# Writing the loop over units of edges out in full in a graph-convolution kernel

## What is computed

```
h   = x @ W_in2f
Wij = ssp(f_ij @ W_filt1 + b_filt1) @ W_filt2 + b_filt2      # f_ij: 200000 x 20
Wij = Wij * rcut_ij[:, None]
agg = segment_sum(h[idx_j] * Wij, idx_i, num_segments=6250)  # idx_j = dst (sorted), idx_i = src
out = ssp(agg @ W_out1 + b_out1) @ W_out2 + b_out2           # ssp(v) = softplus(v) - log 2
return layernorm(x + out)
```

## Time and profile before

| | |
|---|---|
| median of three runs | 2365.92 us |
| the profiled execution | 2370.19 us, of which the span is 2368.4 us |
| PE busy | 2142.1 us, 90% |
| POOL busy | 1862.0 us, 79% |
| DVE, ACT busy | 1670.5 us (71%), 1660.6 us (70%) |
| stretch of the units on POOL | 125.9 us to 2274.6 us |
| DMA | 250.00 MB, mean 106 GB/s |

### The profile page before, as it was taken

The page is one execution under the profiler, slowest core; times in us unless marked ns, Lnnn a source line. Parts: engine busy times, 40 slices in busy tenths (PEclk is TensorE's granted clock), DMA queues, the critical chain, the costliest instruction groups (busy, mean ns, idle before and its releaser), DMA issues.

```text
span 2368.4 us, 60320 instructions
## 1 busy us (share of the span) xinstructions
PE 2142.1 (90%) x16313; PEld 1410.6 (60%) x16313; DVE 1670.5 (71%) x3879; ACT 1660.6 (70%) x3725; POOL 1862.0 (79%) x1174
## 2 busy tenths in 40 slices
PE   2488999999999999999999999999999999999936
PEld 1365666566666666666666566666666666666613
DVE  5467777768676777767777777777777777777726
ACT  0277777678687777777776777877777777777616
POOL 2078888888888888888888888888888888888874
PEclk8599999999999999999999999999999999999978
DMA  6776665666666666666666666656666566666574
GB/s 208 267 155 95 96 95 90 93 90 100 94 99 92 100 97 95 92 98 97 93 98 93 94 94 94 102 94 96 96 98 91 93 100 95 95 96 91 68 159 130
DMA packets 370945, 250.00 MB, mean 106 GB/s; under 512 B 88788, under 2 KB 350143, under 8 KB 370315
## 3 DMA queue, kind: packets, MB, share of 16 engines
q0 software_dynamic: 160560, 73.14, 32.7%
q1 hardware_dynamic: 199482, 155.27, 27.3%
q10 hardware_dynamic: 10476, 16.77, 1.9%
HBM read 149.90 MB, written 95.13 MB: 103 GB/s over the span
## 4 chain that ended last, share of the span: by engine, by line
DMA 43%; PE 19%; POOL 17%; issue 14%; DVE 3%; ACT 3%; POOLq 0%; SPq 0%; DVEq 0%; ACTq 0%
DMA table<-total,index 40%; POOL table L732 16%; PE unit_psum L1872 5%; PE unit_psum L1891 4%; PE both_psum L1828 3%; PE total_psum L1841 2%; PE pre_psum L1815 2%; DMA h_parts<-h_out 1%; DMA src_g<-in_src 1%; PE both_psum L1853 1%; PE both_psum L1824 1%; ACT out_rows L1122 1%; DVE rank L1249 0%; DVE rank_part L1244 0%; POOL half_sum L776 0%
## 5 line engine op out<-in xcount | busy, mean ns | idle before, releaser
L732 POOL DMA_INDIRECT table<-total,index x1115 | 1803.3, 1617 | 444.8 <-issue 249.0
L1872 PE MATMUL unit_psum<-moving,route_hot 128*128 128x386 bf16 x3136 | 608.8, 331 | 41.0 <-ACT ring L915 36.9
L885 ACT ACTIVATE h_dst<-both_psum,cols 128x128 f32<-128x128 f32 x1564 | 450.2, 386 | 102.4 <-PE both_psum L1853 99.0
L1891 PE MATMUL unit_psum<-scat_hot,ring 64*128 64x448 bf16 x4704 | 481.7, 353 | 9.2 <-DVE scat_hot L1432 6.5
L1872 PEld LDWEIGHTS unit_psum<-moving,route_hot 128*128 128x128 bf16 x3136 | 295.0, 99 | 266.9 <-ACT ring L915 108.2
L915 ACT ACTIVATE ring<-unit_psum 128x386 bf16<-128x386 f32 x784 | 373.5, 509 | 111.8 <-PE unit_psum L1872 70.5
L1828 PEld LDWEIGHTS both_psum<-w_f,hidden 128*128 128x128 f32 x3128 | 415.3, 193 | 18.3
L1828 PE MATMUL both_psum<-w_f,hidden 128*128 128x128 f32 x3128 | 415.7, 276 | 0.0
L1891 PEld LDWEIGHTS unit_psum<-scat_hot,ring 64*128 64x128 bf16 x4704 | 217.0, 95 | 218.5 <-DVE acc_t L1448 7.7
L849 ACT ACTIVATE soft<-pre_psum 128x1024 f32<-128x1024 f32 x196 | 201.9, 1030 | 169.5 <-PE pre_psum L1815 168.6
L1841 PE MATMUL total_psum<-message,same 128*128 128x129 f32 x2232 | 309.5, 281 | 4.8 <-DVE message L1360 4.3
(11 more groups left out here) (116 smaller groups left out, 1599.7 us busy)
## 6 DMA issues: line engine op xcount, KB each, us to landing
dst_b<-dst SPq DMA_DIRECT2D x391, 128.0 KB
src_b<-src SPq DMA_DIRECT2D x279, 128.0 KB
f_t<-in_f_t SPq DMA_DIRECT2D x98, 256.0 KB
table<-total,index POOLq DMA_INDIRECT x1115
table<-zeros ACTq DMA_DIRECT2D x20, 640.0 KB, 5.7
window<-h_parts SPq DMA_DIRECT2D x391, 32.0 KB
parts<-table SPq DMA_DIRECT2D x48, 256.0 KB, 5.2
h_parts<-h_out SPq DMA_DIRECT2D x12, 384.0 KB, 5.4
```

Of the source, the lines that this page charges most:

```text
L732: pool.indirect_dma_start(tables[table], bass.IndirectOffsetOnAxis(index[:, i, k:k + 1], 0), total[:, i, k, 0:DIM], None, compute_op=ALU.a ...
L885: last = act.activation(h_dst[:, b, d], source, ACT.Copy, scale=cols[:, g[1] // HALF % 2, weight:weight + 1])
L1872: last = pe.matmul(unit_psum[:, k % 2, 0:MOVING], route_hot[:, tile, k * P:(k + 1) * P], moving[:, tile, :], start=(tile == 0), stop=(tile ...
L1891: last = pe.matmul(unit_psum[:, strip, 0:BUCKET], ring[rows, r[1] % RING, slot_tile(m), part * DIM:(part + 1) * DIM], scat_hot[rows, r[1] ...
```

## The change

Only the narrow form's control flow is changed. A new helper `run_all` steps through all groups with plain numbers, and `run_units` calls `unit` for all whole units (-1 to 15) before `rest`. No operation on data, no buffer and no semaphore is changed, nor the order of any engine's work. The general form keeps its loop, as do the loops of the setup.

```
-        def run_units(eng, unit, rest):
-
-            for u in range(-1, PEELED):
+        def run_all(step):
+
+            for i in range(-3, GROUPS + 4):
+                step((0, i))
+
+        def run_units(unit, rest):
+
+            for u in range(-1, UNITS - 1):
                 unit((0, u * UNIT))
-            with eng.Fori(0, LOOPS) as j:
-                unit((j, PEELED * UNIT))
             rest()
...
             with sp.If(is_narrow):
-                run_groups(sp, step_narrow)
+                run_all(step_narrow)
...
             with pool.If(is_narrow):
-                run_groups(pool, step_narrow)
+                run_all(step_narrow)
...
             with act.If(is_narrow):
-                run_units(act, unit, rest)
+                run_units(unit, rest)
...
             with dve.If(is_narrow):
-                run_units(dve, unit, rest)
+                run_units(unit, rest)
...
             with pe.If(is_narrow):
-                run_units(pe, unit, rest)
+                run_units(unit, rest)
```

## The result

The changed kernel takes 2375.51 us (median of six, 2374.37 to 2382.2) against 2366.59 us: 1.005 of before, 95% interval 1.0035 to 1.0064. The medians differ by 9 us; f1, the same pair on another chip, gives 1.0051 and 12 us. I had forecast 2361.8 us. The case that came true is my second rival, in kind and in sign, though not in size nor in its spread over all scatters.

A forecast was written before the change was run, and what follows sets the result against it. POOL, saturated by scatters with a fixed gap, was taken as the bound; -4.1 us for its late starts and zero for all else gave 2365.92 - 4.1 = 2361.8 us, range 2352 to 2376 us.

The forecast's parts named there:

- second rival: Neighbours press harder on POOL's scatters without branch pauses: all 952 go to 1.643 us, costing 23.4 us, total 2385.2 us; 12%.
- The bound: POOL is saturated by its scatters, with a fixed 0.305 us gap before each; PE is close behind.
- first rival: PE is the bound after all: all 32.5 us of its branch stalls come back, 2333.4 us; 6%.
- (a): PE's 13 branches back, 32.5 us of stalls: all go, but count only by what POOL lost.
- (b): POOL's five late starts after PE's branches: -4.1 us, bounds 0 and -4.5 us.
- (c): POOL's own branch and register work on its sequencer: zero, hidden behind the running scatter.
- (d): Registers and separate waits on PE, ACT, DVE and SP: zero, what there is lies off the path.
- (e): Fetching the program: bytes go with instructions executed, 80 bytes each; zero, bounds 0 to -1 us.
- (f): Mean duration of POOL's 952 scatters in the passes, 1.619 us: change taken as 0, since neighbours keep their work.
- The order of issue: In the second rival: some VectorE operations lock GpSimd out of a shared port pair, depending on who issues first.

The follow-up runs named there:

- e4: Changed kernel with eight register loads as branchless pauses at the 13 unit boundaries on PE, ACT and DVE: 2368.82 us, 1.0017 of the kernel before.
- e3: Kernel before with SP and POOL written out in full, PE, ACT and DVE keeping their loops: 2364.48 us, 0.9992 of before.
- g3: Kernel before, with loops, its DVE comparison `same` made as four single-input operations, nothing left out: 2339.18 us, 0.9872 of before.
- g4: Changed kernel with the comparison `same` made as four single-input operations, nothing left out: 2327.94 us, 0.9843 of the kernel before.
- f4: Changed kernel with two DVE subtractions shrunk to 2 columns a tile from unit 2, most of their work left out: 2338.48 us, 0.987 of before.
- g1: Kernel before, with loops, the two DVE subtractions shrunk to 2 columns a tile from unit 2: 2330.69 us, 0.9851 of before.
- f3: Changed kernel with eight register loads as pauses at the 13 unit boundaries on PE alone: 2372.33 us, 1.0015 of the kernel before.

## Why the prediction was wrong

- **The bound** was right. POOL works without a break in every run, its gap stays 0.30 us, and 45 us of idle time on PE (e4) cost nothing. The first rival is refuted.
- **(a), PE's branch,** was right as a stall and as something off the path: 32.5 us vanished from PE and came back as waits for ACT, which waits for POOL. ACT's wait grew by 89 us, not by the 25 us that I gave.
- **(b), POOL's late starts,** was half right. POOL's idle time before scatters fell by 1.8 us and not by 4.1 us: the five late starts behind branches are gone, and two new ones, away from the boundaries, have come:

```profile
971.78 1.54 POOL L735 DMA_INDIRECT table<-total,index  x1 [0.86 <-DMA table<-total,index]
...
1346.05 1.55 POOL L735 DMA_INDIRECT table<-total,index  x1 [1.25 <-DMA table<-total,index]
```

- **(c),** the zero for POOL's own branch and registers, holds: e3 is 0.9992 (0.9977 to 1.0007). **(d) and (e),** the zeros for the other engines' registers and for the fetch, were not run by themselves; nothing here speaks against them. The working of (e) was wrong: the bytes do not go with the instructions executed. They are 3.43 MB for 52614 instructions, 65 bytes each and not 80.
- **(f), the scatter's mean,** is the step that failed. I took 0 because "all neighbours keep their work". They did, to within 2 us on DVE. What changed is when that work begins: 256 scatters instead of 211 start while one of the three DVE operations with two SBUF inputs runs, and those take 0.26 us more than the others. The mean in the units 2 to 15 went from 1.619 to 1.635 us; 952 times 0.016 is 15 us. The profiled execution is only 12 us longer, since what follows its last scatter happened to be 3.5 us shorter. My second rival said that the pauses keep scatters short, and had the straight unit, at 1.643 us, as its witness. It put the rise on all 952 scatters; measured, it lies at the boundaries. Its price for the mean, 23.4 us, was too high by half, and its 12% too low: I read the one contrary pass of the earlier trace rows as refuting it, but that pass has scatters as long as the straight unit's, and single passes spread by 3 us. The straight unit is also not the only one without a branch: the first unit has none either, with 1.60 us.
- What I should have asked is which neighbours, and when they begin. The two long scatters in the earlier trace rows, at 302.35 and 304.67 us, had a name beside them in the same trace: a DVE subtraction with two SBUF inputs that began 0.08 and 0.20 us before each:

```profile
302.27 0.68 DVE L1388 TENSOR_TENSOR rest_r<-message_r,moving 128x512 f32<-128x512 f32 x1
...
304.47 0.67 DVE L1396 TENSOR_TENSOR moving<-rest_r,moving 128x512 bf16<-128x512 f32 x1
```

The Trainium skill's page "SBUF — State Buffer", section Who interferes with whom, says that a VectorE instruction with two SBUF inputs contends with a GpSimd instruction that reads SBUF. g3, g4, f4 and g1 agree: 27 to 48 us for making such operations single-input or small. The order of issue, which the prediction named, shows as well: scatters that start during such an operation are the longer ones, and those under which one begins later are not. The same page of the Trainium skill infers that such an operation does not hold up descriptor writing; for these indirect DMAs, whose row numbers lie in SBUF, the measured times decide against carrying that over. The port itself shows in no trace here. Two inputs are not the only form that lengthens, as `route_hot` shows.

What stays open is why DVE's work at a boundary falls into step with the scatters in straight code. That it does is measured: at 11 of 13 boundaries in two executions, at none in the kernel before, and at none in g4 and its repetition, the straight code that is not slower. ACT's 119 waits for adds to land, against 80, would tie the others to POOL's beat, but no run separates this. A pause or a branch at the boundary breaks the step at most places (e3, e4, f3). It does not work by moving the operations into POOL's idle time: those are 6 us of late starts in all, and the two subtractions shown above lie beside scatters in both kernels.

**A better kernel.** g4, the changed kernel with the single-input comparison, leaves nothing out and takes 0.9843 and, repeated, 0.9845 of the kernel before. It beats the same edit in loop form (0.9872, 0.9874).

## What to carry to other kernels

Here an engine that was idle for the same 0.305 us before nearly every instruction was the bound, at a busy share of 79%. Then the price that counts is the mean duration of its instruction. So look at what runs as the long ones start before calling a change of timing elsewhere free: the same work, begun at another moment, made the difference. Taking stalls from an engine that is not the bound can cost time by moving its work onto the bound's. Whether a branch stall matters depends on where the bound stands: here straight code was 9 to 12 us slower with slow scatters, equal with two small operations, and 8 to 11 us faster once another was made cheap, so such a change is to be timed again after the bound has moved.

## What the runs showed of the hardware

- Indirect adds of 128 rows of 512 bytes take 1.54 us on POOL at least, with a gap of 0.305 us between most of them, in all 18 profiled executions.
- One that starts while a DVE operation with two SBUF inputs runs takes 1.82 us on average instead of 1.57 us (211 and 904 scatters of the kernel before). One that starts under an operation of the same length with one SBUF and one PSUM input takes 1.55 us (104 scatters). One under which a two-input operation begins 0.1 to 1.0 us after its start takes 1.56 us (172 scatters). Under a uint16 to bf16 operation with one SBUF input, 0.47 us long (`route_hot`), it takes 1.69 us (80 scatters).
- Four single-input operations in place of one with two inputs took 46 us more DVE time and gave 48 us back in straight code (g4), 27 us in the loop form (g3).
- A taken branch back over the body of a unit costs PE 2.50 us (2.1 to 3.8) and ACT 3.0 us on average in this kernel, straight code none. Eight loads of a word from SBUF into a register pause PE by 45.0 / 13 = 3.5 us (e4).
